# Gated cross-attention block with eight experts on one core: routing of the second batch entry in eight pieces with PSUM operands, gated bias added to the residual ahead, outputs of the first entry weighted on ScalarE and VectorE and added on GpSimd

## The chip, the core and the metric

The kernel runs on one core of one Trainium2 chip. A core has five engines that each work through their own queue in order and meet by semaphores: TensorE (PE in the rows; its weight loads are PEld), VectorE (DVE), ScalarE (ACT), GpSimd (POOL) and SyncE (SP), which here issues DMAs. SBUF is the memory that all engines but TensorE write, PSUM is the one into which TensorE writes; GpSimd does not touch PSUM in this program. The metric is the device time of one execution in microseconds, median over runs.

## What is computed

For x of 2 entries x 512 tokens x 128, and a context of 2 x 32 x 128:

```
ln  = layernorm(layernorm(x)) * g + b           # latents; ctx is normalised once
q   = ln @ Wq ; k, v = [ctx_n ; ln] @ Wkv       # 16 heads of 64, rms-normed q and k
o   = softmax(q k^T / 8 over ctx and x) v       # context keys masked
x1  = x + tanh(g_xattn) * (o @ Wout + bout)
x2  = layernorm(x1)
p   = softmax(x2 @ router)                      # 8 experts
w   = softmax(top2(p)) spread over the experts
out = x1 + tanh(g_ffn) * sum_e w_e * (silu(x2 Wg_e) * (x2 Wu_e)) Wd_e     # F = 256
```

All is float32 at the interface. The large products are made as three fp16 or bf16 products of high and low halves.

## The kernel before

The kernel is written out by hand: each engine has one function, and all of them walk the same slots. 64 attention slots (n = -4 to 67 with the ramps) compute one 256-key part of one head each; then 32 expert slots follow (`expert_slot`, each engine's own). Expert slot n is half of the hidden width (128 of 256) of expert e for one batch entry: slots 0 to 15 are the first entry (experts 0 to 7, two slots each), slots 16 to 31 the second.

One expert slot: TensorE makes gate and up (`gate_up(n)`, lines 1502 to 1504, 3 matmuls of 512 columns each) into one of two PSUM pairs `scores`; ScalarE takes tanh of the gate (L785); VectorE multiplies twice (L1143, L1147), which gives silu(gate) * up and frees `scores`; ScalarE copies that to fp16 (L790) one slot later, GpSimd subtracts to get the low half (L587), and TensorE multiplies by the down weights (`down(n - 2)`, L1517 to L1521) in slot n + 2, behind gate and up of that slot, into one of two banks `o_ps`. When both slots of an expert are down, VectorE adds the weighted result into x1 (which is `x_sb`) with four scalar_tensor_tensor of 128x128 (L1163), scaled by the expert's weight in `w_tok`. TensorE may not reuse the `o_ps` bank before.

In the slots 2 to 5 the last four turns of the attention output of the second entry (`turn_o`, L1216; copied back by ScalarE, L693) and in 3 to 6 its projection (`project_o`, L1233) are mixed in, in 4 to 7 its residual on VectorE (`residual`, L986 and L987, then mean and variance L808, L812), in 7 to 11 its second layernorm: GpSimd's power (L449), ScalarE's z (L699, four of 128x128), TensorE's transposes (L1241), copies (L704, L706, L1001), logits (L1249). The first entry goes through the same in attention slots 49 to 64.

Routing (`route(b, phase)`) is a chain of small VectorE instructions with two exps on ScalarE (L712): softmax of the logits, the largest, the second largest, their weights. Each waits for the one before. Tables say in which slot each phase runs: the first entry in attention slots 64 and 65 and expert slots 0 and 1, the second in expert slots 11 to 14. Operands lie in SBUF: `rt` (in the tile `squares`) holds 128x32, `rs` holds 128x4. In their slots ScalarE takes the exps behind tanh and copy of the slot, and waits there if VectorE has not got so far.

In the attention, GpSimd makes the low halves of the probabilities (L563, 128x1024) and the inverse rms (L460); VectorE the maxima (L905) and the normalised output `o_sb` (L1090).

## Time and profile before

| | us |
|---|---|
| median of three runs | 365.03 (364.54 to 367.39) |
| the profiled execution, own time | 364.97 |
| its span in the profile | 363.2 |
| attention slots 16 to 48, one per | about 3.2 |
| expert slots 18 to 31, one per | 1.96 |

The time of the execution is 1.8 us more than the span. In rows of the time line the first number is the start in microseconds from the start of the span, the second the length, then engine, line of the kernel, operation, tiles written and read, count, and in brackets how long the engine stood idle before and who released it. Matmuls are pipelined: a row of 0.38 us whose next starts 0.22 later occupies TensorE for 0.22.

### The profile page before, as it was taken

To read this page: it belongs to the slowest core of one execution; us is meant where nothing else is said; L and a number is where in the kernel's file an instruction comes from. 1 tells how busy PE (TensorE), PEld (TensorE's weight loads), DVE (VectorE), ACT (ScalarE), POOL (GpSimd) and SP (SyncE) were. 2 spreads that over 40 slices of the span, in tenths; PEclk is the share of its full clock that TensorE was granted. 3 is DMA by queue.
4 is the path that set the end of the run, shared out by engine and by line. 5 is a ranking of instruction groups with operands and counts; after the bars stand their busy time and mean duration, and the time that the engine had idled before them with its cause. 6 is when DMAs were issued, how large, how long until landed. Compare 5 with 4: busy or idle time off the path is not lost.

```text
span 363.2 us, 9207 instructions
## 1 busy us (share of the span) xinstructions
PE 311.7 (86%) x3554; PEld 191.7 (53%) x3577; DVE 290.3 (80%) x585; ACT 195.4 (54%) x332; POOL 255.6 (70%) x199
## 2 busy tenths in 40 slices
PE   0656666799999999999999999999996999769993
PEld 0233232256555565555565556687874665436562
DVE  4797948798998898888898976945538988889994
ACT  2554644477645656555665645466663436245551
POOL 8799864588988888887987987456862355235562
PEclk9996759899999999999999999999999999989997
DMA  6406100801602604405306239430000000001001
GB/s 179 122 1 147 32 4 5 175 9 25 157 9 51 133 7 94 92 4 124 66 4 149 37 104 193 126 119 3 2 2 2 0 2 3 1 0 31 2 3 30
DMA packets 31470, 20.38 MB, mean 56 GB/s; under 512 B 11650, under 2 KB 30914, under 8 KB 31426
## 3 DMA queue, kind: packets, MB, share of 16 engines
q1 hardware_dynamic: 30482, 19.75, 23.7%
...
q10 hardware_dynamic: 944, 0.04, 0.2%
...
HBM read 5.87 MB, written 0.52 MB: 18 GB/s over the span
## 4 chain that ended last, share of the span: by engine, by line
PE 58%; issue 12%; DVE 12%; POOL 12%; ACT 4%; DMA 1%; POOLq 0%; DVEq 0%
PE big L1420 8%; PE big L1421 7%; POOL p_lo L587 7%; PE o_ps L1256 5%; PE o_ps L1257 5%; PE o_ps L1262 5%; PE big L1281 5%; PE tv L1269 4%; PE pj L1233 3%; PE pj L1194 2%; PE tv L1216 1%; PE pj L1192 1%; POOL rms_r L460 1%; PE o_ps L1475 1%; DVE p L1143 1%
## 5 line engine op out<-in xcount | busy, mean ns | idle before, releaser
L563 POOL TENSOR_TENSOR p_lo<-p 128x1024 f16<-128x1024 f32 x64 | 120.6, 1899 | 20.5 <-ACT p L721 20.4
L721 ACT ACTIVATE p<-big 128x1024 f32<-128x1024 f32 x64 | 65.5, 1024 | 58.1 <-PE big L1421 58.1
L905 DVE TENSOR_REDUCE nm_main<-big 128x2 f32<-128x1024 f32 x64 | 78.2, 1222 | 16.6 <-PE big L1281 16.0
L460 POOL TENSOR_TENSOR rms_r<-meansq,power 128x8 f32<-128x8 f32 x32 | 52.3, 1637 | 28.6 <-DVE meansq L880 27.7
L587 POOL TENSOR_TENSOR p_lo<-p,p_lo 128x512 f16<-128x512 f32 x32 | 37.0, 1158 | 47.2 <-ACT p_lo L790 44.8
L1420 PE MATMUL big<-w 128*128 128x512 f16 x128 | 49.1, 383 | 1.4 <-ACT p L721 1.4
L1421 PE MATMUL big<-w 68*128 68x512 f16 x128 | 48.9, 382 | 0.0
L1256 PEld LDWEIGHTS o_ps<-v,p 128*128 128x128 bf16 x512 | 35.6, 99 | 9.2 <-issue 3.9
L1256 PE MATMUL o_ps<-v,p 128*128 128x65 f16 x512 | 40.3, 193 | 0.0
L1257 PE MATMUL o_ps<-v,p 128*128 128x64 f16 x512 | 40.2, 194 | 0.0
L1257 PEld LDWEIGHTS o_ps<-v,p 128*128 128x128 bf16 x512 | 34.1, 97 | 5.3
L1281 PE MATMUL big<-hl 64*128 64x512 f16 x128 | 26.0, 403 | 7.6 <-DVE nm_main L905 6.7
L1517 PE MATMUL o_ps<-wd_hi,p_lo 128*128 128x128 f16 x128 | 23.6, 222 | 9.1 <-POOL p_lo L587 6.8
L785 ACT ACTIVATE p<-big 128x512 f32<-128x512 f32 x32 | 19.0, 594 | 20.2 <-PE big L1504 20.1
L876 DVE TENSOR_REDUCE sumsq<-squares 128x8 f32<-128x512 f32 x32 | 21.6, 676 | 6.6 <-ACT squares L616 6.6
L1143 DVE SCALAR_TENSOR_TENSOR p<-p,big 128x512 f32<-128x512 f32 x32 | 21.8, 681 | 5.6 <-ACT p L785 5.5
L1502 PE MATMUL big<-x2T_hi,gu_hi 128*128 128x512 f16 x64 | 24.5, 383 | 1.9 <-DVE p L1147 1.9
L1262 PE MATMUL o_ps<-v,p_lo 128*128 128x65 f16 x512 | 26.0, 193 | 0.0
L1281 PEld LDWEIGHTS big<-hl 64*128 64x128 f16 x128 | 6.2, 93 | 34.9 <-issue 25.3
L1504 PE MATMUL big<-x2T_hi,wqkv_hl 128*128 128x512 f16 x64 | 24.6, 385 | 0.0
L1503 PE MATMUL big<-x2T_lo,gu_hi 128*128 128x512 f16 x64 | 24.5, 383 | 0.0
L790 ACT CAST p_lo<-p 128x512 f16<-128x512 f32 x32 | 19.6, 613 | 7.5 <-DVE p L1147 7.5
...
## 6 DMA issues: line engine op xcount, KB each, us to landing
...
k1c<-kc_hl SPq DMA_DIRECT2D x32, 8.0 KB, 2.1
```

The lines of the kernel that those rows point to most:

```text
L460: nc.gpsimd.tensor_tensor(rms_r[:, tau % QT, :], meansq[:, tau % QT, :], power[:, 0:8], ALU.pow).then_inc(rr_ok, 1)
L563: nc.gpsimd.tensor_tensor(p_lo[m % NP][:, :], p[m % NP][:, :], p_hi[m % NP], ALU.subtract).then_inc(plo_ok, 1)
L587: nc.gpsimd.tensor_tensor(hid_lo[m % NH], hid[m % NH], hid_hi[m % NH], ALU.subtract).then_inc(hlo_ok, 1)
L721: nc.scalar.activation(p[n % NP][:, :], st_ps, ACT.Exp).then_inc(exp_ok, 1)
L905: nc.vector.tensor_reduce(nm_main[:, u % 2, 2 * c:2 * c + 2, q], s2_ps.rearrange("p (k n) -> p k n", k=2), AX_X, ALU.max, negate=True).the ...
L1143: nc.vector.scalar_tensor_tensor(out=h, in0=h, scalar=1.0, in1=scores[n % 2][:, 0:512], op0=ALU.add, op1=ALU.mult).then_inc(gt_ok, 1)
L1256: nc.tensor.matmul(o_of(q), ph[:, c], vh, start=start and q == 0, stop=False, skip_group_check=True)
L1257: nc.tensor.matmul(o_of(q)[:, 0:DH], ph[:, c], vl, start=False, stop=False, skip_group_check=True)
L1262: last = nc.tensor.matmul(o_of(q), pl[:, c], vh, start=False, stop=True, skip_group_check=True)
L1281: last = nc.tensor.matmul(s2_ps[:, 512 * r:512 * (r + 1)], HL[u % 2][rows, 0, c, q * P:(q + 1) * P], HL[u % 2][rows, 0, 2 + c, :], start=T ...
L1420: nc.tensor.matmul(o, w1[:, 2 + h // 2, h % 2, keys], w1[:, h // 2, h % 2, :], start=True, stop=False)
L1421: last = nc.tensor.matmul(o, w2[0:M_ROWS, 2 + h // 2, h % 2, keys], w2[0:M_ROWS, h // 2, h % 2, :], start=False, stop=True)
```

## The change

Three edits. First, routing: eight phases instead of four, at most three or four instructions each. The first entry's run in attention slots 64 and 65 (phases 0; 1 and 2) and expert slots 0 to 3 (3 and 4; 5; 6; 7), the second's in slots 11 to 18. The copy of the logits to SBUF is gone. For the second entry all 128x32 operands but three (4, 8, 14) and three of the 128x4 (1, 5, 6) lie in PSUM, in the bank `tv`. The second exp is taken in the slot of phase 5: slot 1 for the first entry, slot 16 for the second.

Second, bias: ScalarE multiplies the bias row by tanh(g_xattn) in attention slot 17, GpSimd adds it to x in slots 19 and 27, and the residual is then one scalar_tensor_tensor from PSUM instead of an addition and one.

Third, the first entry's expert outputs: for even experts ScalarE scales o_ps by the weight into `ys` (128x512 f32 in SBUF, four activations), for odd ones VectorE does it with one tensor_tensor; GpSimd adds `ys` to x1. Both come in slot 2e + 4. The bank o_ps is free for TensorE when `ys` is written. The second entry's outputs are added as before.

```diff
-        x1_t = sb("x1_t", [P, 2, D], F32)
-        rt = squares[:, :, :].rearrange("p k c -> p (k c)").rearrange("p (s t e) -> p s t e", s=16, t=T)
-        rs = sb("rs", [P, 8, T], F32)
+        rt = [squares[:, k, :].rearrange("p (s t e) -> p s t e", s=16, t=QT) for k in range(2)]
+        rt_ps = tv[:, :].rearrange("p (s t e) -> p s t e", s=16, t=QT)
+        rs = [sb(f"rs{k}", [P, 8, QT], F32) for k in range(2)]
...
         scores = [s2_ps, st_ps]
+        ys = [p[NH][:, 512 * k:512 * (k + 1)] for k in range(2)]
         x_in, ctx_inn, gains_in, x_in2 = sem("x_in"), sem("ctx_inn"), sem("gains_in"), sem("x_in2")
...
+        BIAS_AT = {19: 0, 27: 1}
...
-        ROUTE_AT = {64: 0, 65: 1}
+        ROUTE_AT = {64: (0,), 65: (1, 2)}
...
-        ROUTE_X0, ROUTE_X1 = {0: 2, 1: 3}, {11 + k: k for k in range(4)}
+        ROUTE_X0, ROUTE_X1 = {0: (3, 4), 1: (5,), 2: (6,), 3: (7,)}, {11 + k: (k,) for k in range(8)}
+        def routed(b, k):
+            return rt_ps[:, k + 1] if b and k not in (4, 8, 14) else rt[b][:, k]
+        def routed_v(b, k):
+            if b and k in (1, 5, 6):
+                return rt_ps[:, 5].rearrange("p t e -> p (t e)")[:, k * QT:(k + 1) * QT]
+            return rs[b][:, k, :]
+        def weighted_by_dve(e):
+            return e % 2 == 1
...
+                if n in BIAS_AT:
+                    b = BIAS_AT[n]
+                    pool.wait_ge(gb_ok, 1)
+                    pool.wait_ge(z1_ok, QT)
+                    tok = slice(b * QT, (b + 1) * QT)
+                    nc.gpsimd.tensor_tensor(x_sb[:, tok, :], x_sb[:, tok, :],
+                                            bout_b[:, :].unsqueeze(1).broadcast_to([P, QT, D]), ALU.add).then_inc(xb_ok, 1)
...
+                m = n - 3
+                if is_xslot(m) and m % FC == FC - 1 and expert_of(m)[1] == 0:
+                    e = expert_of(m)[0]
+                    if weighted_by_dve(e):
+                        pool.wait_ge(ysd_ok, e // 2 + 1)
+                    else:
+                        pool.wait_ge(ysa_ok, e // 2 + 1)
+                    if e == 0:
+                        pool.wait_ge(x1_ok, QT)
+                    need(pool, yp_ok, e)
+                    nc.gpsimd.tensor_tensor(x1[:, 0:QT, :], x1[:, 0:QT, :], ys[e % 2].rearrange("p (t d) -> p t d", t=QT),
+                                            ALU.add).then_inc(yp_ok, 1)
...
+                if n == 17:
+                    act.wait_ge(rest_in, 16 * 3)
+                    act.wait_ge(gate_ok, 1)
+                    nc.scalar.activation(bout_b[:, :], bout_b[:, :], ACT.Copy, scale=gates_t[:, 0:1]).then_inc(gb_ok, 1)
...
+                m = n - 3
+                if is_xslot(m) and m % FC == FC - 1 and expert_of(m)[1] == 0 and not weighted_by_dve(expert_of(m)[0]):
+                    e = expert_of(m)[0]
+                    act.wait_ge(d_mm, m + 1)
+                    if e == 0:
+                        act.wait_ge(w_ok, 1)
+                        act.wait_ge(pv_ok, SLOTS)
+                    need(act, yp_ok, e - 1)
+                    for k in range(QT):
+                        last = nc.scalar.activation(ys[e % 2][:, k * D:(k + 1) * D], o_ps[e % 2][:, k * D:(k + 1) * D],
+                                                    ACT.Copy, scale=w_tok[:, k, e:e + 1])
+                    last.then_inc(ysa_ok, 1)
+                for b, at in enumerate((ROUTE_X0, ROUTE_X1)):
+                    if n in at and 0 in at[n]:
+                        route_exp(b, 0)
+                    if n in at and 5 in at[n]:
+                        route_exp(b, 1)
...
                 dve.wait_ge(y_mm, 2 * t + 2 if t < QT else 2 * QT + t + 1)
-                link(nc.vector.tensor_tensor(x1_t[:, t % 2, :], y_bank(t), bout_b[:, :], ALU.add))
-                nc.vector.scalar_tensor_tensor(out=x1[:, t, :], in0=x1_t[:, t % 2, :], scalar=gates_t[:, 0:1],
+                if t % QT == 0:
+                    dve.wait_ge(xb_ok, t // QT + 1)
+                nc.vector.scalar_tensor_tensor(out=x1[:, t, :], in0=y_bank(t), scalar=gates_t[:, 0:1],
                                                in1=x_sb[:, t, :], op0=ALU.mult, op1=ALU.add).then_inc(x1_ok, 1)
...
-                tok = slice(b * QT, (b + 1) * QT)
                 fall = falling[:, :].unsqueeze(1).broadcast_to([P, QT, E])
+                lg = logits(b).rearrange("p (t e) -> p t e", t=QT)
...
                     return v(k).unsqueeze(2).broadcast_to([P, QT, E])
                 if phase == 0:
                     dve.wait_ge(logit_ok, QT * (b + 1))
-                    rlink(nc.vector.tensor_copy(r(3), logits(b).rearrange("p (t e) -> p t e", t=QT)))
-                    rlink(nc.vector.tensor_reduce(v(0), r(3), AX_X, ALU.max))
-                    nc.vector.tensor_tensor(r(0), r(3), over(0), ALU.subtract).then_inc(rt_exp_in, 1)
+                    rlink(nc.vector.tensor_reduce(v(0), lg, AX_X, ALU.max))
+                    nc.vector.tensor_tensor(r(0), lg, over(0), ALU.subtract).then_inc(rt_exp_in, 1)
                 if phase == 1:
                     dve.wait_ge(rt_exp, 2 * b + 1)
                     rlink(nc.vector.tensor_reduce(v(1), r(1), AX_X, ALU.add))
                     rlink(nc.vector.reciprocal(v(2), v(1)))
                     rlink(nc.vector.tensor_tensor(r(4), r(1), over(2), ALU.mult))
...
+                if phase == 2:
+                    rlink(nc.vector.tensor_reduce(v(3), r(4), AX_X, ALU.max))
+                    rlink(nc.vector.tensor_tensor(r(5), r(4), over(3), ALU.is_ge))
+                    rlink(nc.vector.tensor_tensor(r(6), r(5), fall, ALU.mult))
                 if phase == 3:
+                    rlink(nc.vector.tensor_reduce(v(0), r(6), AX_X, ALU.max))
+                    rlink(nc.vector.tensor_tensor(r(7), r(6), over(0), ALU.is_equal))
+                    rlink(nc.vector.scalar_tensor_tensor(out=r(8), in0=r(7), scalar=-2.0, in1=r(4), op0=ALU.mult,
+                                                         op1=ALU.add))
+                if phase == 4:
+                    rlink(nc.vector.tensor_reduce(v(6), r(8), AX_X, ALU.max))
+                    rlink(nc.vector.tensor_tensor(r(9), r(8), over(6), ALU.is_ge))
+                    rlink(nc.vector.tensor_tensor(r(10), r(9), fall, ALU.mult))
+                if phase == 5:
+                    rlink(nc.vector.tensor_reduce(v(7), r(10), AX_X, ALU.max))
+                    rlink(nc.vector.tensor_tensor(r(11), r(10), over(7), ALU.is_equal))
+                    nc.vector.tensor_tensor(v(4), v(6), v(3), ALU.subtract).then_inc(rt_exp_in, 1)
+                if phase == 6:
                     dve.wait_ge(rt_exp, 2 * b + 2)
                     rlink(nc.vector.tensor_scalar(v(0), v(5), 1.0, None, ALU.add))
                     rlink(nc.vector.reciprocal(v(1), v(0)))
                     rlink(nc.vector.tensor_scalar(v(2), v(1), gates_t[:, 1:2], 0.5, ALU.mult, ALU.mult))
+                if phase == 7:
                     rlink(nc.vector.tensor_tensor(v(7), v(2), v(5), ALU.mult))
...
                 m = n - 3
-                if is_xslot(m) and m % FC == FC - 1:
-                    e, half, _ = expert_of(m)
+                if is_xslot(m) and m % FC == FC - 1 and expert_of(m)[1] == 0 and weighted_by_dve(expert_of(m)[0]):
+                    e = expert_of(m)[0]
+                    dve.wait_ge(d_mm, m + 1)
+                    need(dve, yp_ok, e - 1)
+                    nc.vector.tensor_tensor(ys[e % 2].rearrange("p (t d) -> p t d", t=QT),
+                                            o_ps[e % 2][:, :].rearrange("p (t d) -> p t d", t=QT),
+                                            w_tok[:, 0:QT, e:e + 1].broadcast_to([P, QT, D]), ALU.mult).then_inc(ysd_ok, 1)
+                if is_xslot(m) and m % FC == FC - 1 and expert_of(m)[1] == 1:
+                    e = expert_of(m)[0]
                     i = m // FC
                     dve.wait_ge(d_mm, m + 1)
...
                     pe.wait_ge(o_ok, HG * UNITS)
-                    pe.wait_ge(rt_step, 1)
+                    pe.wait_ge(rt_exp_in, 1)
...
-                    need(pe, y_ok, QT * (i - 1))
+                    if 2 <= i < E + 2:
+                        if weighted_by_dve(i - 2):
+                            pe.wait_ge(ysd_ok, (i - 2) // 2 + 1)
+                        else:
+                            pe.wait_ge(ysa_ok, (i - 2) // 2 + 1)
+                    need(pe, y_ok, QT * (i - 1 - E))
```

VectorE in expert slots 12 to 14, before: the second entry's routing from the answer of the first exp on. `squares` and `rs` are SBUF tiles, `tv` a PSUM bank, `p<-p,big` the two multiplies of an expert slot.

```order
L1034 TENSOR_REDUCE rs<-squares 128x4 [waits rt_exp]
L1035 RECIPROCAL rs<-rs 128x4 [waits rt_step]
L1036 TENSOR_TENSOR squares<-squares,rs 128x32 [waits rt_step]
L1041 TENSOR_REDUCE rs<-squares 128x4 [waits rt_step]
L1042 TENSOR_TENSOR squares<-squares,rs 128x32 [waits rt_step]
L1043 TENSOR_TENSOR squares<-squares,falling 128x32 [waits rt_step]
L1044 TENSOR_REDUCE rs<-squares 128x4 [waits rt_step]
L1045 TENSOR_TENSOR squares<-squares,rs 128x32 [waits rt_step]
L1049 SCALAR_TENSOR_TENSOR squares<-squares 128x32 [waits rt_step]
L1163 SCALAR_TENSOR_TENSOR x_sb<-o_ps,w_tok,x_sb 128x128 [waits y_ok,d_mm,rt_step]
L1163 SCALAR_TENSOR_TENSOR x_sb<-o_ps,w_tok,x_sb 128x128 [waits y_ok] x3
L1143 SCALAR_TENSOR_TENSOR p<-p,big 128x512 [waits th_ok]
```

The same engine and place after the change:

```order
L1092 TENSOR_REDUCE tv<-tv 128x4 [waits rt_exp]
L1093 RECIPROCAL rs<-tv 128x4 [waits rt_step]
L1094 TENSOR_TENSOR squares<-tv,rs 128x32 [waits rt_step]
L1204 SCALAR_TENSOR_TENSOR p<-p,big 128x512 [waits th_ok,rt_step]
L1208 TENSOR_TENSOR p<-p,big 128x512 [waits u_mm,gt_ok]
L1097 TENSOR_REDUCE rs<-squares 128x4
L1098 TENSOR_TENSOR tv<-squares,rs 128x32 [waits rt_step]
L1099 TENSOR_TENSOR tv<-tv,falling 128x32 [waits rt_step]
L1204 SCALAR_TENSOR_TENSOR p<-p,big 128x512 [waits th_ok,rt_step]
L1208 TENSOR_TENSOR p<-p,big 128x512 [waits u_mm,gt_ok]
L1101 TENSOR_REDUCE rs<-tv 128x4
L1102 TENSOR_TENSOR tv<-tv,rs 128x32 [waits rt_step]
```

Nine routing instructions and the head of four weighted additions stood between two pairs of multiplies; now three do, and all but those of `squares` have an operand in PSUM.

ScalarE in expert slots 8 and 9, before: z of the second entry, then tanh (`p<-big`) and copy (`p_lo<-p`) of slot 9, and the two copies of the turned rows.

```order
L699 ACTIVATE z<-x_sb,ln_t,ln_r 128x128 [waits z2b_ok]
L699 ACTIVATE z<-x_sb,ln_t,ln_r 128x128 x3
L785 ACTIVATE p<-big 128x512 [waits hlo_ok,g_mm]
L790 CAST p_lo<-p 128x512 [waits d_mm,hid_ok]
L704 COPY o_sb<-tv 128x512 [waits z2T_ok]
L706 CAST x2T_hi<-o_sb 128x512 [waits x2T_ok]
```

After:

```order
L743 ACTIVATE z<-x_sb,ln_t,ln_r 128x128 [waits z2b_ok]
L743 ACTIVATE z<-x_sb,ln_t,ln_r 128x128 x3
L853 ACTIVATE p<-o_ps,w_tok 128x128 [waits yp_ok,d_mm]
L853 ACTIVATE p<-o_ps,w_tok 128x128 x3
L832 ACTIVATE p<-big 128x512 [waits hlo_ok,g_mm]
L837 CAST p_lo<-p 128x512 [waits d_mm,hid_ok]
L748 COPY o_sb<-tv 128x512 [waits z2T_ok]
L750 CAST x2T_hi<-o_sb 128x512 [waits x2T_ok]
```

Four activations that weight the output of expert 2 have come between z and the tanh of slot 9.

GpSimd in the expert slots, before: low halves (`p_lo<-p,p_lo`) and in slot 7 the power and shift of the second layernorm.

```order
L587 TENSOR_TENSOR p_lo<-p,p_lo 128x512 [waits hhi_ok] x3
L587 TENSOR_TENSOR p_lo<-p,p_lo 128x512 [waits d_mm,hhi_ok] x4
L449 TENSOR_TENSOR ln_r<-ln_v,power 128x4 [waits var_ok]
L553 TENSOR_TENSOR ln_t<-moments,ln_r 128x4 [waits lnr_ok]
L554 TENSOR_SCALAR ln_t<-ln_t 128x4 [waits ln1_step]
L587 TENSOR_TENSOR p_lo<-p,p_lo 128x512 [waits d_mm,hhi_ok] x25
```

After, from the low half of slot 0 to that of slot 9 (`x_sb<-x_sb,p` is the addition of `ys`):

```order
L619 TENSOR_TENSOR p_lo<-p,p_lo 128x512 [waits hhi_ok] x3
L619 TENSOR_TENSOR p_lo<-p,p_lo 128x512 [waits d_mm,hhi_ok]
L632 TENSOR_TENSOR x_sb<-x_sb,p 128x512 [waits x1_ok,ysa_ok]
L619 TENSOR_TENSOR p_lo<-p,p_lo 128x512 [waits d_mm,hhi_ok] x2
L632 TENSOR_TENSOR x_sb<-x_sb,p 128x512 [waits yp_ok,ysd_ok]
L619 TENSOR_TENSOR p_lo<-p,p_lo 128x512 [waits d_mm,hhi_ok]
L474 TENSOR_TENSOR ln_r<-ln_v,power 128x4 [waits var_ok]
L578 TENSOR_TENSOR ln_t<-moments,ln_r 128x4 [waits lnr_ok]
L579 TENSOR_SCALAR ln_t<-ln_t 128x4 [waits ln1_step]
L619 TENSOR_TENSOR p_lo<-p,p_lo 128x512 [waits d_mm,hhi_ok]
L632 TENSOR_TENSOR x_sb<-x_sb,p 128x512 [waits yp_ok,ysa_ok]
L619 TENSOR_TENSOR p_lo<-p,p_lo 128x512 [waits d_mm,hhi_ok] x2
```

From expert 0 on an addition stands behind every second low half, and the next low half waits for it in order.

## Rows read from the trace of the kernel before

**Rows 1.** The page, part 1: busy us, share of the span, instructions.
```profile
PE 311.7 (86%) x3554; PEld 191.7 (53%) x3577; DVE 290.3 (80%) x585; ACT 195.4 (54%) x332; POOL 255.6 (70%) x199
```

**Rows 2.** Windows: length, busy per engine (count), PE clock, DMA share, GB/s.
```profile
276.00:300.00 24.00, 20.47 (x177) 14.50 (x178) 21.34 (x56) 11.29 (x22) 9.57 (x10) 1.00 0.00 1
300.00:326.00 26.00, 20.32 (x160) 11.74 (x158) 22.31 (x59) 11.78 (x26) 9.51 (x9) 0.93 0.00 1
326.00:360.00 34.00, 30.61 (x291) 18.65 (x289) 30.22 (x70) 17.14 (x31) 19.42 (x17) 0.99 0.04 10
```

**Rows 3.** Time line, PE: one slot of the second half, gate to next gate.
```profile
329.61 0.38 PE L1502 MATMUL big<-x2T_hi,gu_hi 128*128 128x512 f16 x1
...
330.90 0.22 PE L1517 MATMUL o_ps<-wd_hi,p_lo 128*128 128x128 f16 x1
...
331.57 0.38 PE L1502 MATMUL big<-x2T_hi,gu_hi 128*128 128x512 f16 x1
```

**Rows 4.** Time line of ACT, DVE, POOL and PEld: the chain in those slots.
```profile
330.45 0.60 ACT L785 ACTIVATE p<-big 128x512 f32<-128x512 f32 x1 [0.86 <-PE big L1504]
330.95 0.61 ACT L790 CAST p_lo<-p 128x512 f16<-128x512 f32 x1
...
329.12 0.69 DVE L1143 SCALAR_TENSOR_TENSOR p<-p,big 128x512 f32<-128x512 f32 x1 [0.44 <-ACT p L785]
329.84 0.69 DVE L1147 TENSOR_TENSOR p<-p,big 128x512 f32<-128x512 f32 x1
330.44 1.12 DVE L1163 SCALAR_TENSOR_TENSOR x_sb<-o_ps,w_tok,x_sb 128x128 f32<-128x128 f32 x4
331.48 0.68 DVE L1143 SCALAR_TENSOR_TENSOR p<-p,big 128x512 f32<-128x512 f32 x1
...
331.63 1.16 POOL L587 TENSOR_TENSOR p_lo<-p,p_lo 128x512 f16<-128x512 f32 x1 [0.80 <-ACT p_lo L790]
...
332.84 0.10 PEld L1517 LDWEIGHTS o_ps<-wd_hi,p_lo 128*128 128x128 f16 x1 [0.31 <-POOL p_lo L587]
```

**Rows 5.** Time line, PE: gate/up starts of slots 5, 11, 14, 16, 17, 21.
```profile
288.37 0.38 PE L1502 MATMUL big<-x2T_hi,gu_hi 128*128 128x512 f16 x1
...
304.52 0.38 PE L1502 MATMUL big<-x2T_hi,gu_hi 128*128 128x512 f16 x1
...
312.33 0.38 PE L1502 MATMUL big<-x2T_hi,gu_hi 128*128 128x512 f16 x1
...
320.99 0.38 PE L1502 MATMUL big<-x2T_hi,gu_hi 128*128 128x512 f16 x1
...
325.07 0.39 PE L1502 MATMUL big<-x2T_hi,gu_hi 128*128 128x512 f16 x1
...
333.54 0.38 PE L1502 MATMUL big<-x2T_hi,gu_hi 128*128 128x512 f16 x1
```

**Rows 6.** Time line, ACT: the second exp of each routing.
```profile
277.95 0.20 ACT L712 ACTIVATE rs<-rs 128x4 f32<-128x4 f32 x1 [4.55 <-DVE rs L1047]
...
317.83 0.20 ACT L712 ACTIVATE rs<-rs 128x4 f32<-128x4 f32 x1 [5.88 <-DVE rs L1047]
```

**Rows 7.** Groups by line and form, DVE: busy us, mean ns, idle before.
```profile
L987 DVE SCALAR_TENSOR_TENSOR x_sb<-x_t,gates_t,x_sb 128x128 f32<-128x128 f32 x8 | 4.1, 508 | 0.3
L986 DVE TENSOR_TENSOR x_t<-pj,bout_b 128x128 f32<-128x128 f32 x8 | 2.3, 284 | 3.8 <-PE pj L1233 3.8
```

**Rows 8.** Time line, DVE and POOL: a routing instruction beside a low half.
```profile
312.09 1.14 DVE L1042 TENSOR_TENSOR squares<-squares,rs 128x32 f32<-128x32 f32 x1
313.26 0.19 DVE L1043 TENSOR_TENSOR squares<-squares,falling 128x32 f32<-128x32 f32 x1
...
312.03 1.15 POOL L587 TENSOR_TENSOR p_lo<-p,p_lo 128x512 f16<-128x512 f32 x1 [0.43 <-ACT p_lo L790]
```

**Rows 9.** Time line, PE and DVE: waits beside the first entry's residual.
```profile
233.16 0.37 PE L1297 MATMUL o_ps<-mask_row,ones_row 1*128 1x512 bf16 x1 [0.69 <-DVE o_sb L1090]
...
247.58 0.40 PE L1475 MATMUL o_ps<-w,k1c 128*32 128x512 f16 x4 [0.47 <-DVE o_sb L1090]
...
245.43 0.87 DVE L987 SCALAR_TENSOR_TENSOR x_sb<-x_t,gates_t,x_sb 128x128 f32<-128x128 f32 x1
```

**Rows 10.** Time line, POOL and PE: attention slots 18 to 21.
```profile
128.88 3.75 POOL L563 TENSOR_TENSOR p_lo<-p 128x1024 f16<-128x1024 f32 x2
133.58 1.64 POOL L460 TENSOR_TENSOR rms_r<-meansq,power 128x8 f32<-128x8 f32 x1 [0.95 <-DVE meansq L880]
...
135.12 0.41 PE L1262 MATMUL o_ps<-v,p_lo 128*128 128x65 f16 x8
```

**Rows 11.** Time line, ACT: four activations of 128x128 (z).
```profile
299.91 1.65 ACT L699 ACTIVATE z<-x_sb,ln_t,ln_r 128x128 f32<-128x128 f32 x4
```

54 lines of the change are left out of this document (19 added, 35 removed).

## Prediction, made before the changed kernel was run

> **What bounds the kernel now.** I read the page's busy shares first: TensorE 86%, VectorE 80%, GpSimd 70% [rows 1]. No engine is full, so the question is where TensorE waits. The stretches show it [rows 2]: in 326 to 360 TensorE is busy 30.61 of 34 us, but in 276 to 326, which holds expert slots 2 to 17, it is busy 20.47 + 20.32 = 40.8 of 50 us while VectorE is busy 43.7. About 9 us of the expert stage are TensorE waiting behind VectorE or behind ScalarE and GpSimd that VectorE holds up. I number the 32 expert slots from 0; a slot is six gate and up matmuls and then the twelve down matmuls of two slots earlier.
>
> In the undisturbed second half a slot takes 331.57 - 329.61 = 1.96 us, with no gap [rows 3]. Its chain is [rows 4]: gate/up at T = 329.61, tanh at T + 0.84, the fp16 copy 0.50 behind it, GpSimd's low half 0.68 later (1.16 long), and 1.21 after GpSimd's start the weight load of the down matmul may begin; the row of that load waits 0.31 us for GpSimd, but the matmuls run on. So there is nearly no slack here: a low half that is late by x makes TensorE late by about x. VectorE needs 0.72 + 0.60 us for a slot's two multiplies and 1.04 for four weighted adds, 3.7 us for two slots against 3.93 on TensorE.
>
> In the first 18 slots that balance is broken. ScalarE stands in a routing exp for 4.55 and 5.88 us while tanh is queued behind it [rows 6], and gate/up starts at 288.37 (slot 5), 304.52 (slot 11), 312.33 (slot 14), 320.99 (slot 16) and 333.54 (slot 21) [rows 5]: slots 14 to 16 take 8.66 us instead of 3.9.
>
> **The change part by part.**
>
> Residual. Each of 8 tiles loses one addition (0.284 us and the wait, together 0.32), and its STT reads PSUM instead of two SBUF tiles (508 ns on average, 0.87 at 245.43, to some 0.35) [rows 7, 9]. In the attention this matters at two places only, where TensorE waits for o_sb behind the residual: 0.69 us at 233.16 and 0.47 at 247.58 [rows 9]. At the first 0.32 comes off, at the second 0.33 + 0.52 are saved and all 0.47 goes: **-0.8**.
>
> Bias. One ScalarE multiply (about 0.4 us) lies in ScalarE's idle time. Two GpSimd additions of 128x512, some 1.2 us each, follow the first of two low halves in slots 19 and 27. There GpSimd runs two low halves in one stretch (3.75 us from 128.88) and the second, ready at 132.63, is used at 135.12: 2.5 us of cover; behind it GpSimd sits idle 0.95 us [rows 10]. Cost 0; if the cover were gone, at most 1.2 each.
>
> Routing of the first entry. It has one instruction less and is spread over more slots. The second exp moves from slot 0 to slot 1, behind tanh 1: so tanh 1 no longer waits, but tanh 2 does, for VectorE's pieces 3 to 5. Two of those pieces' instructions read SBUF twice and fall on GpSimd's low half of slot 0: the like of them at 312.09 took 1.14 us instead of the 0.19 of its neighbour, ending as GpSimd's did [rows 8]. I walked the queues with the latencies above: the low half starts at 277.3, the piece stands until 278.4, the exp runs at 280.7, tanh 2 at 280.8, gate/up 5 at 288.4, as before. Gain before slot 5: 0. If the collision is missed, 0.9.
>
> The Trainium skill, SBUF — State Buffer, section Who interferes with whom, says that a Vector instruction with two SBUF inputs contends with a GpSimd instruction that reads SBUF and that whoever starts first keeps the pair. The row at 312.09 agrees, and by that rule PSUM operands free the second entry's routing, while added GpSimd work makes a collision likelier elsewhere.
>
> Weighting of the first entry. VectorE loses 32 STTs (eight groups of 1.04 us = 8.3) and gains four multiplies of 128x512 with a PSUM input, 0.69 long and 0.62 to the next, as the gate multiply in [rows 4]: -5.8 us. ScalarE gains four groups of four 128x128, 1.65 us a group by the group of z at 299.91 [rows 11]. GpSimd gains eight additions of 128x512. No row has an addition with f32 result; the nearest with two inputs and 512 columns is 1.16 us [rows 4]; bounds 1.0 and 1.9 (a low half of 1024 columns, half of 3.75 [rows 10]). I take 1.2, since it is 512 columns. The Trainium skill, GPSIMD Engine Reference, section 3.1, gives 4497 ns for an f32 addition of 2048 columns, 1.1 us for 512 as an estimate; the sum would be 0.5 less by it.
>
> What these cost: both new steps stand in order. In slot 2e + 4 ScalarE does tanh, copy, then 1.6 us of weighting, so the next tanh, due 1.96 later, is late; GpSimd waits for the weighted product before it takes the next low half, and that one is late by 0.7 to 1.9 us, which by [rows 4] TensorE pays unless another wait covers it. Walking slot by slot:
> - slots 5 to 9: e = 0 and 1 are covered by the projections still in these slots; residual and the missing weighted adds bring gate/up 9 forward by 0.8;
> - slots 8 to 11: z of the second entry (1.65) and weighting of e = 2 (1.6) follow each other on ScalarE; tanh 9 comes at 302.6, the low half of slot 8 starts at 303.9 behind the addition. Gate/up 11 at 305.7 against 304.52: **+1.2**;
> - slots 11 to 14: e = 3 and 4 keep that distance, gate/up 14 at 313.1 against 312.33;
> - slots 14 to 16: the routing in pieces of three takes 0.66 between gates and no exp stands in front of tanh 14; gate/up 16 at 317.6 against 320.99: **-3.4**, of which the addition of e = 5 has taken 0.8 already;
> - slots 16 to 21: second exp behind the weighting of e = 6 costs nothing more. Without the stall of slot 16 (4.08 us to 325.07) the lead grows to 4.6; addition 7 waits for VectorE's multiply behind the last routing piece, and the low half of slot 18 starts 1.7 late. Gate/up 21 at 330.6 against 333.54: **-2.9** in all, with 0.2 of it from the routing's first piece, which no longer waits for GpSimd.
>
> From there both kernels run at 1.96 us a slot. Sum: -0.8 - 2.9 = -3.7. The profiled execution took 364.97 us (span 363.2), the median of the three runs is 365.03, so nothing is to be corrected: 361.3, and I say 361.4.
>
> **Rivals.**
> A, the added work eats the gain. If an addition takes 1.9 us instead of 1.2, six of the eight lie in front of a low half that TensorE waits for: 6 x 0.7 = 4.2 back, 365.5. With additions of 1.5, 363.2. For it: GpSimd's slack is nearly nil [rows 4]. Against it: the 1.16 of the nearest row. 363.3 to 366.5.
> B, slower: ScalarE and GpSimd in order become the bound of the first half. Before, 9 us were lost; if each of the eight experts loses what slot 10 loses in my walk (1.9 us), 15.2 are lost, 6.2 more, less the attention's 0.8: 370.4. It decides from the point where weighting and addition together take over 4 us, more than two slots (1.65 and 1.2 by my prices). Against it: GpSimd's load of two slots is 3 x 1.2 = 3.6 us, below 3.93.
> C, more gain: the collision in slot 0 is missed (-0.9) and GpSimd's waits in slots 10, 14 and 18 are half as long (-2): 358.5. For it: my walk adds latencies where the chip may overlap.
> D, the change does not do what it says: PSUM operands are no faster or collide as before. One instruction of the new second routing alone still reads SBUF twice; a stall of 1.1 us on two pieces gives back 2: 363.4, within A's range.
>
> **How the numbers follow.** The forecast, 359.3 to 363.3, has 0.56; A and D 0.25; B 0.11; C 0.08. The range leaves out B and most of C: 359.0 to 366.0. About 1% (3.65 us, so 361.4 and 368.7) is what a measurement of this kernel can tell from no change. The forecast lies on that edge: somewhat over half of its 0.56 falls below 361.4 if its errors are even, and with C that makes 0.40 faster; within 1% are the rest of the forecast, A, D and the light end of B, 0.51; slower 0.09.
>
> **What would show it.** In the changed profile: waits of TensorE at L1297 and L1475's places gone or at 0.3; the exp of slot 1 preceded by about 3 us of idle ScalarE; GpSimd's additions at 1.1 to 1.3 us each, and several low halves started only when an addition ended; gate/up 11 later than before, gate/up 16 three us earlier; no routing instruction of the second entry over 0.3 us but the one that compares r(4). I am wrong if GpSimd's additions take over 1.6 us, or if the first stretch up to slot 11 is already some us ahead, or if the second half runs slower than 1.96 a slot.

## The result, and the profile after

The changed kernel took 360.52 us (median of 4 runs, 359.9 to 361.2) against 365.01 for the kernel before beside it: ratio 0.986 with a 95% interval of 0.982 to 0.991. The profiled execution took 361.07 us, its span is 359.2. The prediction was 361.4 (359.0 to 366.0). The changed kernel was run again, in a later session, beside the last experiments: 360.57 (6 runs) against 365.51, ratio 0.987 (0.983 to 0.991).

First the busy line of the changed kernel's page and the three stretches, as in [rows 1, 2] (length, then busy time of each engine with its count, PE clock, DMA share, GB/s):

```profile
PE 312.3 (87%) x3577; PEld 191.7 (53%) x3577; DVE 277.2 (77%) x547; ACT 199.9 (56%) x349; POOL 266.9 (74%) x209
```

```profile
276.00:300.00 24.00, 21.51 (x181) 14.83 (x181) 19.19 (x47) 12.59 (x27) 12.91 (x13) 1.00 0.00 1
300.00:326.00 26.00, 23.11 (x205) 14.13 (x205) 19.77 (x48) 17.25 (x41) 17.87 (x16) 1.00 0.01 2
326.00:360.00 34.00, 25.57 (x242) 15.53 (x239) 26.03 (x59) 14.00 (x25) 17.39 (x15) 0.95 0.06 16
```

In 276 to 326 TensorE is busy 21.51 + 23.11 = 44.6 of 50 us, before 40.8, and VectorE 39.0, before 43.7. ScalarE (29.8 us, before 23.1) and GpSimd (30.8, before 19.1) have taken over more than VectorE lost. The expert stage's gain lies in these two stretches. What TensorE still waits for in the expert stage is one view: its waits in 271 to 335 (engine, tile, line, releaser; total us, times, longest), before:

```profile
PE o_ps L1517 <- POOL p_lo L587: 4.6, 4, 2.2
PE o_ps L1517 <- DVE x_sb L1163: 2.3, 2, 1.6
PE big L1502 <- DVE p L1147: 1.9, 3, 1.1
PE pj L1233 <- DVE x_sb L987: 0.4, 1, 0.4
```

and after:

```profile
PE o_ps L1591 <- POOL p_lo L619: 4.1, 3, 1.5
PE big L1570 <- DVE p L1208: 1.8, 2, 0.9
PE pj L1301 <- ACT o_sb L737: 0.8, 1, 0.8
PE pj L1301 <- DVE x_sb L1048: 0.4, 1, 0.4
```

The 2.3 us for VectorE's weighted additions are gone; 4.1 us for GpSimd's low halves stay. In the attention (214 to 271) TensorE's waits for VectorE were 0.7 and 0.5 us before [rows 9]; after there is one:

```profile
PE big L1488 <- ACT p L764: 0.6, 2, 0.4
PE o_ps L1365 <- DVE o_sb L1154: 0.4, 1, 0.4
```

**How runs are compared below.** Up to the attention exp of slot 17 all kernels here run the same code, but their profiled executions reach that exp between 120.58 and 124.50 us. TensorE's granted clock differs ahead of it: 0.67 to 0.85 in the stretch 50 to 70 us, 0.87 to 1.00 in 70 to 98. So besides the median I give two intervals of the profiled execution: A, from the attention exp of slot 17 to the first gate matmul of the experts, and X, from there to the gate matmul of slot 22. From slot 22 on every kernel runs at 1.96 to 1.97 us a slot. The changed kernel is the only one profiled twice, in two sessions: X is 59.91 both times, A 149.82 and 149.85. All other values of A and X are of one execution each. The median of the kernel before was 365.01, 365.44, 365.27 and 365.51 in the four sessions; each ratio is to that of its own session.

| gate matmul of slot, us after slot 0 | before | after | residual alone | routing alone | weighting alone | residual + routing | after, addition later |
|---|---|---|---|---|---|---|---|
| 4 | 12.45 | 12.61 | 12.46 | 12.61 | 12.45 | 12.61 | 12.61 |
| 5 | 16.41 | 16.51 | 15.95 | 16.83 | 16.41 | 16.51 | 16.51 |
| 9 | 27.45 | 26.59 | 26.03 | 27.87 | 27.17 | 26.58 | 26.59 |
| 11 | 32.56 | 33.32 | 31.51 | 32.98 | 33.53 | 32.07 | 33.08 |
| 14 | 40.37 | 40.55 | 39.33 | 40.56 | 41.34 | 39.64 | 40.41 |
| 16 | 49.03 | 44.71 | 47.99 | 45.17 | 49.72 | 44.26 | 44.79 |
| 17 | 53.11 | 48.23 | 52.07 | 47.65 | 54.28 | 46.74 | 46.75 |
| 21 | 61.58 | 57.94 | 60.54 | 57.79 | 62.93 | 56.87 | 56.32 |
| 22 (X) | 63.54 | 59.91 | 62.50 | 60.35 | 64.90 | 59.43 | 58.38 |
| A | 150.69 | 149.82 | 149.86 | 150.78 | 150.77 | 149.87 | 149.82 |

The profiled gain is 0.87 in A and 3.63 in X, 4.50 in all. The medians differ by as much (365.01 - 360.52 = 4.49), the profiled executions themselves by 3.90 (364.97 and 361.07), since the changed one reached the exp of slot 17 0.59 us later.

### The profile page after: what moved, and what is told of

The parts are those of the page before. It is cut to its first block, busy times and chain, and to the rows that moved or that the text cites. A ratio compares the mean times of both kernels' runs of the same rounds, so it can differ in the third digit from the quotient of the medians.

```text
span 359.2 us, 9236 instructions
## 1 busy us (share of the span) xinstructions
PE 312.3 (87%) x3577; PEld 191.7 (53%) x3577; DVE 277.2 (77%) x547; ACT 199.9 (56%) x349; POOL 266.9 (74%) x209
## 4 chain that ended last, share of the span: by engine, by line
PE 59%; POOL 14%; issue 12%; DVE 9%; ACT 4%; DMA 1%; POOLq 0%; DVEq 0%; ACTq 0%
POOL p_lo L619 8%; PE big L1488 8%; PE big L1489 8%; PE o_ps L1324 6%; PE o_ps L1325 5%; PE o_ps L1330 5%; PE big L1349 5%; PE tv L1337 4%; PE pj L1301 3%; PE pj L1261 1%; PE pj L1262 1%; PE pj L1260 1%; POOL rms_r L485 1%; PE tv L1284 1%; PE o_ps L1543 1%
## 5 line engine op out<-in xcount | busy, mean ns | idle before, releaser
L832 ACT ACTIVATE p<-big 128x512 f32<-128x512 f32 x32 | 19.1, 597 | 23.7 <-PE big L1572 23.6
L1593 PE MATMUL o_ps<-wqkv_hl,p_lo 128*128 128x128 bf16 x128 | 23.1, 219 | 0.0
```

## The experiments

### Each edit alone

The kernel before, with the bias and residual edit only:

```diff
-                link(nc.vector.tensor_tensor(x1_t[:, t % 2, :], y_bank(t), bout_b[:, :], ALU.add))
-                nc.vector.scalar_tensor_tensor(out=x1[:, t, :], in0=x1_t[:, t % 2, :], scalar=gates_t[:, 0:1],
+                if t % QT == 0:
+                    dve.wait_ge(xb_ok, t // QT + 1)
+                nc.vector.scalar_tensor_tensor(out=x1[:, t, :], in0=y_bank(t), scalar=gates_t[:, 0:1],
```

> The kernel before with the bias edit alone (ScalarE multiplies the bias row, GpSimd adds it to x in attention slots 19 and 27, one instruction per residual). Theory, the prediction's step: 0.8 us in the attention (the two waits of TensorE beside the residual, 0.69 and 0.47, go to about 0.36 and 0), nothing from GpSimd's two additions, and next to nothing in expert slots 4 to 7, where the projections bound: 364.0 to 364.3 against 365.0. Rival: the gain is absorbed behind the residual and the time stays at 365.0. Rival: the additions on GpSimd are seen and it is slower.

Measured: 363.15 us against 365.44 (ratio 0.993, 0.989 to 0.996); A -0.83, X -1.04. More than I expected. The extra is in slots 4 to 8, and 0.4 of it is given back at slot 9 (3.41 instead of 3.04): slots 4 and 5 take 3.49 and 3.29 us where they took 3.96 and 3.61, because VectorE had no idle time there: a residual tile costs it 0.32 us less (0.47 where its second operation had been slow), and the slot is shorter by as much. And slot 8 falls from 2.61 to 1.97. The time lines of VectorE and GpSimd show a part of the reason (start, length, engine, line, operation). Before:

```profile
297.14 0.90 DVE L995 TENSOR_SCALAR ln_v<-moments 128x4 f32<-128x4 f32 x1
...
296.86 1.16 POOL L587 TENSOR_TENSOR p_lo<-p,p_lo 128x512 f16<-128x512 f32 x1 [1.69 <-ACT p_lo L790]
```

and with the residual edit alone:

```profile
295.40 0.17 DVE L1012 TENSOR_SCALAR ln_v<-moments 128x4 f32<-128x4 f32 x1
...
295.45 1.16 POOL L599 TENSOR_TENSOR p_lo<-p,p_lo 128x512 f16<-128x512 f32 x1 [1.70 <-ACT p_lo L806]
```

A VectorE operation on four columns took 0.90 us and ended with GpSimd's low half when it started 0.28 behind it; started 0.05 ahead of it, it took 0.17. The edit moved it ahead. How much of slot 8's 0.64 is due to that is not shown: with the weighting alone (below) the operation took 0.46 and slot 8 still 2.65.

Routing alone (the edit's phases, slots and PSUM operands; the rest as before):

```diff
-        ROUTE_X0, ROUTE_X1 = {0: 2, 1: 3}, {11 + k: k for k in range(4)}
+        ROUTE_X0, ROUTE_X1 = {0: (3, 4), 1: (5,), 2: (6,), 3: (7,)}, {11 + k: (k,) for k in range(8)}
```

> The kernel before with the routing edit alone (eight pieces, second entry's operands in PSUM); VectorE still adds the first entry's outputs itself. Theory: slots 2 to 5 as before; in slots 11 to 18 VectorE has per two slots 2.64 of gates, 1.04 of weighted additions and 1.3 of routing, 5.0 us, which bounds: 20 us where before 25.1 passed; together with the loss of the stalls about 3.5 us gained, 361.5 (360.8 to 362.5). Rival: the stall is only moved, since VectorE has the same work: 364 to 365.

Measured: 362.00 (ratio 0.990, 0.985 to 0.994), inside the range expected; A +0.09, X -3.19. It carries most of the gain: from gate 14 to gate 16 are 4.61 us instead of 8.66. Up to slot 9 it costs 0.42, in the first entry's pieces. In the kernel before TensorE's granted clock was 0.58 in slot 16, behind its stalls of slots 14 and 15. Nothing of the gain is seen to come from that: the kernel with the residual edit alone stalls as long there (4.33, 4.33 and 4.08 us for slots 14, 15 and 16) and its clock was 1.00 from 271 to 336 us.

Weighting alone:

```diff
+                    for k in range(QT):
+                        last = nc.scalar.activation(ys[e % 2][:, k * D:(k + 1) * D], o_ps[e % 2][:, k * D:(k + 1) * D],
+                                                    ACT.Copy, scale=w_tok[:, k, e:e + 1])
```

> The kernel before with the weighting edit alone (ScalarE and VectorE scale, GpSimd adds); routing and residual as before. Theory: 0.5 to 1 us won by slot 9, given back at slots 10 and 11, where ScalarE has z and weighting one behind the other, and 1.5 to 2 won in slots 12 to 16, where a weighted addition no longer stands beside nine routing instructions: 363 (362.3 to 364). Rival: the weighting carries the whole gain of the change: 361. Rival: GpSimd in order costs more than VectorE's relief: 366.

Measured: 368.60 (366.33 to 371.4; ratio 1.007, 1.003 to 1.011); X +1.36. Slower, so my expectation of 363 fell and the second rival (GpSimd in order costs more than VectorE's relief) holds. TensorE's waits in 271 to 335:

```profile
PE o_ps L1566 <- POOL p_lo L599: 8.7, 7, 2.4
PE big L1545 <- DVE p L1183: 3.1, 3, 1.5
```

The waits for weighted outputs are gone, but those for GpSimd's low halves rose from 4.6 to 8.7 us. In this kernel the additions also run beside the old residual, which reads SBUF twice; its last one, which took 0.35 us before, reads

```profile
295.44 1.27 DVE L1023 SCALAR_TENSOR_TENSOR x_sb<-x_t,gates_t,x_sb 128x128 f32<-128x128 f32 x1
```

beside GpSimd's addition of 295.29. The median is 1.8 us further from before than X accounts for; the profiled execution, at 366.3, was the quickest of the twelve. The slowest, 371.3 to 371.4, had a mean granted clock of 0.951 against its 0.963; where they lost the rest was not seen.

### Without the weighting

> The kernel before with two of the three edits, the one to the attention's residual and the second entry's routing in eight pieces from PSUM; the first entry's outputs stay weighted by VectorE. Theory (a), the edits add up and the weighting on two engines brings nothing (alone it was 368.6 in place of 365.4): the residual's 0.87 + 1.04 and the routing's 3.19 make 365.0 - 5.1 = 359.9 us, range 359.4 to 360.4. Theory (b), that of the prediction (VectorE is relieved of 5.8 us by the weighting and this carries the gain between slots 9 and 21): without it 362.0 to 362.5.

Measured: 360.51 (359.76 to 364.31; ratio 0.988, 0.983 to 0.992), A -0.82, X 59.43. The sum of the two edits alone gives X = 63.54 - 1.04 - 3.19 = 59.31: they add up to within 0.12. And theory (b), which the prediction's credit of 5.8 us to VectorE stands for, is refuted: without the third edit the kernel is as fast as with it (360.51 and 360.52, ratios 0.988 and 0.986), in X even 0.48 faster. TensorE's waits in 271 to 335:

```profile
PE big L1534 <- DVE p L1179: 2.4, 4, 0.9
PE o_ps L1549 <- POOL p_lo L614: 2.2, 4, 1.0
```

VectorE is waited for 2.4 us instead of 1.8, GpSimd 2.2 instead of 4.1: the weighting trades the one for the other. The table has it by slot: with the weighting slots 10, 16 and 20 take 3.33, 3.52 and 3.67 us (2.08, 2.48 and 2.49 without), and slots 15, 17, 18 and 21 are 0.6, 0.6, 1.0 and 0.6 shorter.

### What of GpSimd's addition costs: its place or its length

The place. TensorE's slot 16 in the changed kernel, time lines of VectorE, ScalarE, GpSimd and TensorE:

```profile
316.02 0.69 DVE L1220 TENSOR_TENSOR p<-o_ps,w_tok 128x512 f32<-128x512 f32 x1
...
318.58 1.13 ACT L853 ACTIVATE p<-o_ps,w_tok 128x128 f32<-128x128 f32 x4
...
316.79 1.27 POOL L632 TENSOR_TENSOR x_sb<-x_sb,p 128x512 f32<-128x512 f32 x1 [1.37 <-DVE p L1220]
318.02 2.27 POOL L619 TENSOR_TENSOR p_lo<-p,p_lo 128x512 f16<-128x512 f32 x2
...
319.23 0.23 PE L1591 MATMUL o_ps<-wd_hi,p_lo 128*128 128x128 f16 x1 [1.38 <-POOL p_lo L619]
```

GpSimd sits idle 1.37 us until VectorE has the weighted product, adds for 1.27, and the low half behind it starts at 318.02, while TensorE stands 1.38 us. The same happens at 326.50. So the addition was put one slot later, behind the low half:

```diff
-                m = n - 3
+                m = n - 4
                 if is_xslot(m) and m % FC == FC - 1 and expert_of(m)[1] == 0:
                     e = expert_of(m)[0]
                     if weighted_by_dve(e):
                         pool.wait_ge(ysd_ok, e // 2 + 1)
```

> The changed kernel, with GpSimd's addition of an expert's weighted outputs written one slot later, behind the low half of the next slot instead of ahead of it. Theory (a): what the additions cost is their place in GpSimd's order: in the changed kernel the gate products of slots 17, 21 and 11 start 3.52, 3.67 and 3.33 us after those before them, against 1.97 where nothing waits, with GpSimd's low half late behind an addition each time. With the addition behind it that is gone: 1.55 + 1.70 + a quarter of a microsecond at slot 11 (the rest there is the matrix engine's wait for another thing), less about 1 for what comes due next: 358.0 us, range 357.0 to 359.3. Theory (b), the additions are late because GpSimd has no time left at all between slots 9 and 21, whatever the order: 360.5 as the changed kernel.

Measured: 359.68 (358.36 to 359.88; ratio 0.983, 0.979 to 0.986), X 58.38, that is -1.53. The same slot on GpSimd:

```profile
316.22 1.16 POOL L619 TENSOR_TENSOR p_lo<-p,p_lo 128x512 f16<-128x512 f32 x1 [0.41 <-ACT p_lo L837]
317.34 1.27 POOL L632 TENSOR_TENSOR x_sb<-x_sb,p 128x512 f32<-128x512 f32 x1
```

The low half starts 1.8 us earlier, and slots 16 and 20 take 1.96 and 1.97 instead of 3.52 and 3.67. Theory (a) holds in kind, but more comes due next than I took off: 1.2 us at slot 18 (3.29 instead of 2.10), 0.5, 0.4 and 0.4 at slots 9, 15 and 19 (slot 10 takes 2.58 instead of 3.33). The gain is 1.5 in X. The median moved by 0.8, where I had expected 2.5; below the kernel before of its own session it lies 5.6, the changed kernel 4.5 and 4.9.

The length. The addition cut to 4 columns at the same place, with its waits:

```diff
-                    nc.gpsimd.tensor_tensor(x1[:, 0:QT, :], x1[:, 0:QT, :], ys[e % 2].rearrange("p (t d) -> p t d", t=QT),
-                                            ALU.add).then_inc(yp_ok, 1)
+                    nc.gpsimd.tensor_tensor(x1[:, 0, 0:4], x1[:, 0, 0:4], ys[e % 2][:, 0:4], ALU.add).then_inc(yp_ok, 1)
```

> The changed kernel, with GpSimd's additions cut from 512 to 4 columns at the same places and with the same waits (it leaves the first entry's expert outputs out of the result but for those 4 columns, so its time is one without that work). Theory (a), the length of the addition (1.27 us each, eight of them) holds the low halves up: the low halves behind it end about 1.1 us earlier, gate products 11, 17 and 21 start up to 1.1 earlier each: 358.3 us, range 357.3 to 359.3. Theory (b), it is the waits in GpSimd's order (for the weighted outputs) and not the addition's length: within 0.5 of the changed kernel, 360.0 to 360.5.

Measured: 360.00 (358.4 to 361.16), X 58.53. The median is the one of theory (b); by the interval, -1.38, the truth lies between the two theories. Slots 16 and 20 go to 2.48 and 2.59, about what they take without the weighting, and slot 18 pays 1.1 of it back.

And longer, with one more addition of 256 columns ahead:

```diff
+                    nc.gpsimd.tensor_tensor(spare[:, :], ys[e % 2][:, 0:256], ys[e % 2][:, 256:512], ALU.add)
                     nc.gpsimd.tensor_tensor(x1[:, 0:QT, :], x1[:, 0:QT, :], ys[e % 2].rearrange("p (t d) -> p t d", t=QT),
```

> The changed kernel, with one more GpSimd addition of 256 columns (its result is not used) ahead of each of the eight additions: GpSimd's part of the weighting grows from 1.27 to some 1.9 us an expert. Theory (a), that of the prediction's rival A: six of the eight are in front of a low half that the matrix engine waits for, 6 x 0.65 = 3.9 us: 364.4 us. Theory (b), by the run with 4 columns, only the two or three places at slots 11, 17 and 21 count: 2 or 3 x 0.65 = 1.3 to 2.0: 361.8 to 362.5.

Measured: 365.65 (ratio 0.999, 0.996 to 1.003): the whole gain of the change is gone. X is 64.48, +4.57. The group of the added operation (busy us, mean ns, idle before it):

```profile
L633 POOL TENSOR_TENSOR spare<-p 128x256 f32<-128x256 f32 x8 | 5.8, 728 | 8.0 <-DVE p L1222 4.4 <-ACT p L855 1.9 <-PE o_ps L1597 1.7
```

and TensorE's waits in 271 to 335:

```profile
PE o_ps L1593 <- POOL p_lo L620: 7.4, 6, 2.2
```

TensorE now waits for a low half in six places, slots 8, 10, 12, 14, 16 and 20, where it was three (10, 16 and 20). So theory (a), which is rival A's mechanism, holds in kind, and my reading in (b) that only two or three places count falls. Its size is another matter. 8 x 0.73 = 5.8 us of GpSimd cost 4.57 us, near 6 x 0.73 = 4.4, but 1.66 of the 4.57 lie in slot 17, which takes 3.63 us instead of 1.97. TensorE does not wait there:

```profile
320.61 0.23 PE L1593 MATMUL o_ps<-wd_hi,p_lo 128*128 128x128 f16 x1 [2.06 <-POOL p_lo L620]
...
322.00 0.63 PE L1574 MATMUL big<-x2T_hi,wqkv_hl 128*128 128x512 f16 x1
322.42 0.63 PE L1572 MATMUL big<-x2T_hi,gu_hi 128*128 128x512 f16 x1
...
324.92 0.38 PE L1572 MATMUL big<-x2T_hi,gu_hi 128*128 128x512 f16 x1
```

Behind the wait of 2.06 us the gate and up matmuls start 0.43 apart instead of 0.22; the granted clock is 0.59 in 321 to 323.5, so the lower of its two levels (1.2 GHz and not 2.4) for most of it. In the changed kernel, with waits of 1.38 and 1.54 us, it stays at 1.00; but so it does with the weighting alone, whose longest wait is 2.4 us, so the wait's length by itself does not decide it. Whether the other eleven executions had the same fall is not known; the quickest took 363.26, 1.4 less than the profiled one. The waits themselves cost 2.9: 0.65, 0.69, 0.39, 0.30, 0.67 and 0.72 in the six slots, less 0.5 that slots 11 and 18 are shorter.

The two runs together show two slopes. From 0.20 to 1.27 us an addition costs little (eight times 1.07 us less bring 1.38, or 0.16 us for each), from 1.27 to 2.00 us 0.50 for each, and 0.79 with the fall of the clock in this execution. Where between these three lengths the slope changes is not shown.

### SBUF or PSUM for the second entry's operands

```diff
-            return rt_ps[:, k + 1] if b and k not in (4, 8, 14) else rt[b][:, k]
+            return rt[b][:, k]
```

(and the three 128x4 operands likewise).

> The changed kernel with the second entry's routing operands back in SBUF, all else as changed. GpSimd is busy some 18 of 26 us there. Theory that PSUM operands matter because an instruction with two SBUF inputs stands while GpSimd works: several of the pieces' instructions read 0.4 to 1.3 us instead of 0.2, in sum 3 to 5 us on VectorE, of which VectorE's idle time takes a part: 361.3 to 363, against 360.5 of the changed kernel. Rival: the pieces have slack and PSUM brings nothing: 360.5.

Measured: 362.61 (ratio 0.992, 0.989 to 0.996), X 62.29, +2.38, inside the range expected. VectorE and GpSimd at 318 us:

```profile
317.76 1.06 DVE L1106 TENSOR_TENSOR squares<-squares,rs 128x32 f32<-128x32 f32 x1
318.86 1.08 DVE L1107 TENSOR_TENSOR squares<-squares,falling 128x32 f32<-128x32 f32 x1
...
317.62 2.26 POOL L617 TENSOR_TENSOR p_lo<-p,p_lo 128x512 f16<-128x512 f32 x2
```

The same two operations take 0.20 us each in the changed kernel, with one operand in PSUM. The Trainium skill, SBUF — State Buffer, section Who interferes with whom, says that a Vector instruction with two SBUF inputs and a GpSimd instruction that reads SBUF exclude each other; this pair of runs agrees: each of the two took about a low half's length, 1.06 and 1.08. The same section says that a tensor_scalar can enter modes that take the ports shared with GpSimd; the row of `ln_v` above, an operation with one SBUF input (0.90 beside a low half, 0.17 ahead of one), agrees.

### The first entry's second exp

The changed kernel's second exp of the first entry on ScalarE, with VectorE and GpSimd:

```profile
280.46 0.20 ACT L755 ACTIVATE rs<-rs 128x4 f32<-128x4 f32 x1 [3.50 <-DVE rs L1113]
280.57 0.58 ACT L832 ACTIVATE p<-big 128x512 f32<-128x512 f32 x1
...
277.11 1.13 DVE L1108 TENSOR_TENSOR squares<-squares,rs 128x32 f32<-128x32 f32 x1
...
277.03 1.16 POOL L619 TENSOR_TENSOR p_lo<-p,p_lo 128x512 f16<-128x512 f32 x1 [4.89 <-ACT p_lo L837]
```

As predicted, the piece stands till the low half has ended, and tanh 2 is queued behind the exp. Moved one slot on:

```diff
-        ROUTE_X0, ROUTE_X1 = {0: (3, 4), 1: (5,), 2: (6,), 3: (7,)}, {11 + k: (k,) for k in range(8)}
+        ROUTE_X0, ROUTE_X1 = {0: (3, 4), 1: (5,), 3: (6,), 4: (7,)}, {11 + k: (k,) for k in range(8)}
...
+                if n == 2:
+                    route_exp(0, 1)
```

> The changed kernel, with the first entry's second exponential in ScalarE's slot 2 instead of slot 1 and the two vector operations behind it in slots 3 and 4. Theory (a): the gate function of slot 2 is queued 3.5 us behind an exponential that waits for VectorE, and gate product 4 comes 4.33 us after number 3 because of it; with the exponential one slot later product 4 starts about 1.0 us earlier and the end with it by 0.8: 359.7 us. Theory (b): the first entry's weights come later for it, ScalarE's weighting of expert 0 and GpSimd's first addition wait for them, and what is won at product 4 is given back at product 8: 360.5.

Measured: X 58.43, -1.48: slot 3 takes 3.30 instead of 4.33 us, slot 4 3.48 instead of 3.90, and nothing is given back. In X theory (a) holds, with more than the 0.8 to 1.0 I took. The median, 361.38 (359.35 to 362.99), does not show it. The profiled execution of this kernel lost 2.5 us long before the edit's place, between attention slots 1 and 10. The stretch 70 to 98 of the changed kernel, and of this one (columns as in [rows 2]):

```profile
70.00:98.00 28.00, 27.08 (x354) 15.85 (x353) 24.05 (x41) 19.34 (x32) 24.79 (x16) 1.00 0.31 67
```

```profile
70.00:98.00 28.00, 27.01 (x307) 15.48 (x311) 22.07 (x38) 17.99 (x30) 22.34 (x14) 0.87 0.25 53
```

TensorE's granted clock is 0.87 there instead of 1.00, in code that both kernels share. Of the six times three are from 359.35 to 360.54 and three, this one among them, from 362.21 to 362.99.

### The moves together

> The changed kernel with both moves at once: GpSimd's addition one slot later and the first entry's second exponential one slot later. From the first gate product of the expert stage to the 23rd, the changed kernel takes 59.91 us, the later addition alone 58.38, the later exponential alone 58.43. Theory (a), the two stalls are apart (slots 4 and 5 against slots 11, 17 and 21) and add up: 56.9 us for that stretch, some 357.6 us in all (356.8 to 358.8). Theory (b), what is won at slot 4 is waited for again at slots 11 to 14: 57.6 to 58.4, some 358.5 to 359.7.

Measured: 357.67 (356.66 to 359.55; ratio 0.979, 0.975 to 0.983), X 56.96 for 56.9 expected: the two add up. This is the fastest version, 2.9 us below the changed kernel run beside it and 7.8 below the kernel before.

> The residual's and the routing's edit, VectorE weights all outputs, and the first entry's second exponential one slot later. Theory (a), the weighting on two engines is worth something only once GpSimd's addition stands behind the low half: this kernel takes 59.43 - 1.48 = 57.95 us from gate product 1 to 23, about 359.0 us in all, and the kernel with both moves and the weighting is 1.0 to 1.4 faster than it. Theory (b), the weighting brings nothing in either order: this one is level with the other, 357.6 to 358.2.

Measured: 360.91 (358.89 to 363.4), X 58.85. The later exp brings only 0.58 without the weighting. At slot 3 it brings the same 1.03, but slot 5 takes 4.16 instead of 3.29. VectorE's time line:

```profile
287.15 0.15 DVE L1093 TENSOR_TENSOR rs<-rs 128x4 f32<-128x4 f32 x1
287.33 0.19 DVE L1094 TENSOR_TENSOR squares<-squares,rs 128x32 f32<-128x32 f32 x1
287.56 0.19 DVE L1095 TENSOR_TENSOR squares<-squares,rs 128x32 f32<-128x32 f32 x1
287.79 0.19 DVE L1096 TENSOR_TENSOR w_tok<-squares 128x32 f32<-128x32 f32 x1
288.01 1.13 DVE L1196 SCALAR_TENSOR_TENSOR x_sb<-o_ps,w_tok,x_sb 128x128 f32<-128x128 f32 x4
```

Last piece and weighted additions now stand in one slot of an engine that has no idle time there. So the weighting on two engines is worth 58.85 - 56.96 = 1.89 us in X once the exp and the addition stand later (medians: 3.2, with the clock's scatter in it), 1.05 with the later addition alone (59.43 - 58.38), and -0.48 in the order that the change gave it. Theory (a) holds, though the 1.89 is above its 1.0 to 1.4: this kernel is slower than it said, by the 0.87 at slot 5.

> The changed kernel once more, on the same chip and in the same rounds as the three others, so that they stand against it directly: 360.5 us (359.9 to 361.2), 59.91 us from gate product 1 to 23.

Measured: 360.57 (360.32 to 361.57), X 59.91, as expected.

## Why the prediction was right, and where its steps were not

**The time.** 361.4 predicted, 360.5 measured, inside the forecast's own range (359.3 to 363.3). The parts: attention -0.8 predicted, -0.87 measured; expert stage -2.9 predicted, -3.63 measured.

**Attention, bias.** Right. The wait at the residual's second place is gone and the first is 0.4 us; the additions of the bias took 1.27 us each and A has no trace of them.

**First entry's routing.** The chain was walked right; the gain of 0 before slot 5 is the sum of two errors. Counted from slot 0 (271.96 before, 271.68 after), the piece beside GpSimd's low half ended at 6.56 (walked: 6.44), the exp ran at 8.78 (8.74) and gate/up 5 started at 16.51 (walked: as before, 16.41). But the routing alone puts gate/up 5 at 16.83, 0.42 late, and the residual alone at 15.95, 0.46 early, where the prediction had nothing for either: that they cancel is luck.

**The walk through the slots.** Relative to slot 0, predicted and measured: slot 9 -0.8 and -0.86; slot 11 +1.2 and +0.76; slot 14 +0.8 and +0.18; slot 16 -3.4 and -4.32; slot 21 -2.9 and -3.64. The shape is right, and so is the last stall: the low half of slot 18 was to be 1.7 late, and slot 20 takes 3.67 - 1.97 = 1.70 too long. The term that was mis-sized is "1.65 us a group by the group of z": ScalarE's weighting took 1.10 to 1.15. Rows of the group at the place where z and weighting follow each other:

```profile
299.13 1.65 ACT L743 ACTIVATE z<-x_sb,ln_t,ln_r 128x128 f32<-128x128 f32 x4 [0.76 <-POOL ln_t L579]
300.69 1.10 ACT L853 ACTIVATE p<-o_ps,w_tok 128x128 f32<-128x128 f32 x4
301.68 0.59 ACT L832 ACTIVATE p<-big 128x512 f32<-128x512 f32 x1
```

tanh 9 came 30.0 us after slot 0, where the walk had 30.6. No run changed the weighting's length, so what follows is read from rows. Of the 0.74 us by which slot 21 is earlier than walked, 0.44 is there at slot 11 and 0.62 at slot 14. z was the wrong model: it takes its scale and its bias from tiles, and reads SBUF; the weighting takes one of them from a tile and reads PSUM. The Trainium skill, ScalarE: Activation LUTs, section What ACT_TABLE_LOAD costs, charges each such pointer operand about 93 ns, 0.37 us for four; the trace agrees in direction, and its difference of 0.50 to 0.55 us is larger.

**The additions.** 1.2 us assumed, 1.27 measured; the estimate of 1.1 from the Trainium skill, GPSIMD Engine Reference, section 3.1, was further off than the nearest row's 1.16.

**What carried the gain.** Here the prediction's account was wrong in part, although its sum was right. Its walk gave the 3.4 us between slots 14 and 16 to the routing, and that held. But it credited the weighting with "-5.8 us" of VectorE and charged its costs in the same walk, so it never said what that edit was worth net. The runs do: +1.36 us in X alone, +0.48 on top of the other two, no difference in the medians. That the sum came out with this edit in it owes something to luck. The gain is the routing's (-3.19) and the residual's (-0.83 in A and -1.04 in X; the latter I had counted only as a share of 0.8). "Residual and the missing weighted adds" bring slot 9 forward: the residual alone brings 1.42, the routing's spreading costs 0.42, and with both slot 9 stands where it stands with all three edits (26.58 and 26.59), so the missing adds bring nothing there.

**The rivals.** A's mechanism is real and was near: 2.00 us of GpSimd for each expert instead of 1.27 gives 365.65, a part of it by the lower clock that A did not have. B did not come about, as 1.1 us of weighting and 1.27 of addition are far from the 4 us from which it decides; but for the weighting alone its sign is right (368.60). D: PSUM operands bring 2.38 us in X, against the 2 that D would have given back; only one piece of the second entry was slow, the comparison of r(4), with 0.40 us. C did not come about: the collision in slot 0 took place, and 1.5 of the 2 us that it took off GpSimd's waits come only when the addition stands later.
